# Softmax denominators through DRAM: three wide reciprocals in place of eight narrow ones

## What is computed

```
x = x + 0.5 * ffn(layernorm(x))        # silu(x Wg) * (x Wu), 2 of every 4 kept, Wd
x = x + attn(layernorm(x))
x = x + 0.5 * ffn(layernorm(x))

attn:  32 query heads of 8 channels, 8 key and value heads (4 query heads share one)
  scores = rope(q) . rope(k) / sqrt(8),  -inf above the diagonal
  out = softmax(scores) . v,  then out Wo + bo
```

## Time and profile before

| what | value |
|---|---|
| runs (3) | 810.50, 810.17, 810.17 us; median 810.17 |
| the profiled execution | 806.71 us, span 805.2 us |
| mean granted clock of PE | 0.972 |
| PE busy | 759.5 us (94%) |
| DVE busy | 716.0 us (89%) |
| ACT busy | 488.1 us (61%) |
| POOL busy | 263.5 us (33%) |
| reciprocals L1078 | 8 |

### The profile page before, as it was taken

One profiled execution on the slowest core, in us unless ns is written; L12 is line 12 of the kernel. 1 busy time (PEld: TensorE's weight loads), 2 busy tenths in 40 slices (PEclk: granted clock), 3 DMA queues, 4 the chain that ended last, 5 costly groups with the idle time before them and its releaser, 6 DMA issues.

```text
span 805.2 us, 15466 instructions
## 1 busy us (share of the span) xinstructions
PE 759.5 (94%) x5168; PEld 506.0 (63%) x5168; DVE 716.0 (89%) x1862; ACT 488.1 (61%) x949; POOL 263.5 (33%) x359
## 2 busy tenths in 40 slices
PE   4999999988899999999999999999999999999996
PEld 3787887877655544445444444544444577888886
DVE  4989999987698999999999999999995459989997
ACT  6444443321125888888888878888688544343451
POOL 1143534038732322323322223255235111533330
PEclk9999999999955999999999999999899999999999
DMA  8100000015843113333113332533313000000001
GB/s 303 55 0 1 1 1 1 1 74 179 231 147 68 41 40 75 90 74 71 43 41 75 76 73 48 141 71 78 76 35 74 14 7 1 1 27 1 27 1 52
DMA packets 21966, 48.60 MB, mean 60 GB/s; under 512 B 3744, under 2 KB 8224, under 8 KB 21376
## 3 DMA queue, kind: packets, MB, share of 16 engines
q1 hardware_dynamic: 21824, 47.56, 22.7%
q10 hardware_dynamic: 64, 0.07, 0.0%
HBM read 19.63 MB, written 14.16 MB: 42 GB/s over the span
## 4 chain that ended last, share of the span: by engine, by line
PE 64%; DVE 19%; issue 6%; POOL 5%; ACT 4%; DMA 1%; PEldq 0%; PEld 0%; SPq 0%; DVEq 0%; ACTq 0%; POOLq 0%
PE att_o_ps L1393 18%; PE att_s_ps L1377 15%; PE att_m_ps L1348 11%; PE ffn_gate L218 6%; PE ffn_up L218 5%; PE ffn_y_ps L351 5%; DVE ffn_hs L524 3%; DVE ffn_h L566 2%; POOL qkv_turned L859 2%; POOL qkv_parts L864 2%; PE att_m_ps L1356 1%; DVE att_scratch L1442 1%; DVE ffn_rank L510 1%; DVE ffn_pair_max L498 1%; PE out_y_ps L1152 1%
## 5 line engine op out<-in xcount | busy, mean ns | idle before, releaser
L1495 ACT ACTIVATE att_probs<-att_s_ps 128x512 f32<-128x512 f32 (+1 forms) x640 | 311.1, 556 | 66.3 <-PE att_s_ps L1377 64.4
L1348 PE MATMUL att_m_ps<-k,q 64*128 64x512 f32 (+3 forms) x768 | 225.1, 401 | 3.3 <-DVE att_maxima L1442 2.1
L1442 DVE CUSTOM_DVE_ANT_0 att_scratch<-att_m_ps,att_causal 128x512 bf16<-128x512 f32 (+3 forms) x512 | 221.1, 485 | 7.5 <-PE att_m_ps L1348 5.9
L1377 PE MATMUL att_s_ps<-q,k 64*128 64x512 f32 (+3 forms) x768 | 216.2, 387 | 3.3 <-ACT att_probs L1495 1.4
L1377 PEld LDWEIGHTS att_s_ps<-q,k 64*128 64x128 f32 x768 | 121.8, 190 | 101.3 <-ACT att_probs L1495 93.1
L1445 DVE TENSOR_REDUCE att_maxima<-att_m_ps 128x1 f32<-128x512 f32 x256 | 161.5, 681 | 8.0 <-PE att_m_ps L1348 8.0
L1534 POOL TENSOR_SCALAR_AFFINE_SELECT att_probs<-att_probs 128x512 f32<-128x512 f32 x128 | 80.4, 641 | 250.7 <-ACT att_probs L1495 250.7
L1393 PE MATMUL att_o_ps<-att_probs,att_vs 128*32 128x512 f32 (+3 forms) x1536 | 160.3, 505 | 2.0 <-POOL att_probs L1534 1.6
L1348 PEld LDWEIGHTS att_m_ps<-k,q 64*128 64x128 f32 x768 | 128.9, 195 | 44.8 <-DVE att_maxima L1442 25.6
L630 POOL TENSOR_TENSOR ffn_hs_lo<-ffn_hs,ffn_hs_hi 128x512 fp32r<-128x512 f32 x48 | 76.6, 1621 | 106.3 <-ACT ffn_hs_hi L427 106.3
L454 ACT ACTIVATE ffn_a<-ffn_h 128x512 f32<-128x512 f32 x64 | 40.5, 633 | 106.9 <-DVE ffn_h L566 106.9
(11 more groups left out here) (114 smaller groups left out, 1165.0 us busy)
## 6 DMA issues: line engine op xcount, KB each, us to landing
q_rows<-qkv_parts SPq DMA_DIRECT2D x16, 512.0 KB, 3.7
q<-q_rows SPq DMA_DIRECT2D x16, 512.0 KB, 4.6
q<-q SPq DMA_DIRECT2D x16, 512.0 KB, 4.4
k_rows<-qkv_parts SPq DMA_DIRECT2D x8, 256.0 KB, 3.0
k<-k_rows SPq DMA_DIRECT2D x16, 128.0 KB, 5.0
k<-k SPq DMA_DIRECT2D x16, 128.0 KB, 4.5
q<-att_shift_t SPq DMA_DIRECT2D x128, 4.0 KB
out_num<-att_sums SPq DMA_DIRECT2D x128, 16.0 KB
```

The source lines that it names most:

```text
L1348: pe.matmul(m_ps[unit_bank(n)][:, COLUMNS[m]], q[g % 2][m_lane, h, t * P:(t + 1) * P], k[g % 2][m_lane, kc * N:kc * N + cols], start=True, ...
L1377: last = pe.matmul(s_ps[n % S_BANKS][:, at:at + w], k[g % 2][s_lane, kb * P:(kb + 1) * P], q[g % 2][s_lane, h, qc * N + q0:qc * N + q0 + w ...
L1442: dve.tensor_tensor_reduce(out=scratch[bank][:, at], in0=m_ps[bank][:, at], in1=causal[:, N - n:], scale=1.0, scalar=LOWEST, op0=ALU.add, ...
L1495: act.activation(probs[u % len(probs)][:, h, SPAN[u]], s_ps[n % S_BANKS][:, SPAN[u]], ACT.Exp, scale=SCALE).then_inc(exp_done, 1)
```

## The change

The denominators of groups 0 to 11 are stored to a DRAM tensor, den_rows, in place of the SBUF tile. Two periods ahead of their use, in groups 8 and 12, SP waits for the stores of the two groups before, and issues one load that lays the 64 rows over 128 partitions x 256 columns, then the 32 rows over 128 x 128. This stands between the sums of half 0 and the next group's second shift. DVE waits for that load and inverts pieces of 128 columns as before: two behind units 6 and 12 of group 10, one behind unit 6 of group 14. The tensor of inverses has its channel dimension outermost, so that each partition's piece of a row is stored eight times with a stride; the spread reads it in that order.

```diff
@@ -986,7 +986,7 @@
-    def __init__(self, nc, ctx, late, hole, x, wo_rows, inverse_rows, KVH, QPK, HD, T, N, y_banks):
+    def __init__(self, nc, ctx, late, hole, x, wo_rows, den_rows, inverse_rows, KVH, QPK, HD, T, N, y_banks):
         self.x, self.wo_rows, self.KVH, self.QPK, self.HD, self.T, self.N = x, wo_rows, KVH, QPK, HD, T, N
         _, TILES, C = x.shape
@@ -1010,14 +1010,19 @@
         self.wo = [late.take(f"wo_{n}", [P, KT, C], F32R) for n in ("hi", "lo")]
         self.wo_raw = hole.take("wo_raw", [P, KT, C], F32)
-        self.den_rows = hole.take("out_den_rows", [self.HEADS * self.QC + self.PER_K * self.QC, N], F32)
-        self.inverse_rows = inverse_rows
+
+
+        self.den_rows, self.inverse_rows = den_rows, inverse_rows
+        self.ROW_SPANS = [slice(0, self.HEADS * self.QC), slice(self.HEADS * self.QC, (self.HEADS + self.PER_K) * self.QC)]
+        self.den_cols = [(rows.stop - rows.start) * N // P for rows in self.ROW_SPANS]
+        self.den_parts = [hole.take(f"out_den_parts{b}", [P, cols], F32) for b, cols in enumerate(self.den_cols)]
         self.y_ps = y_banks
         self.wo_loaded = sem("wo_loaded")
         self.wo_hi_ready = sem("wo_hi_ready")
         self.wo_lo_ready = sem("wo_lo_ready")
         self.stored = [[sem(f"stored{e}_{qc}") for qc in range(self.QC)] for e in range(2)]
+        self.den_loaded = [sem(f"den_loaded{b}") for b in range(2)]
         self.inverted = sem("inverted")
         self.inverse_stored = sem("inverse_stored")
         self.spread_done = [sem(f"spread_done{b}") for b in range(2)]
@@ -1066,24 +1071,29 @@
             row = self.den_row(b, k, qc) + first
             queue.dma_start(self.den_rows[row:row + self.QPK], sums[qc][HD:P:32]).then_inc(stored, 16)
+    def load_denominators(self, sp, b):
+
+        for g in ((self.KVH - 2, self.KVH - 1) if b == 0 else (self.KVH + self.KVH // 2 - 2, self.KVH + self.KVH // 2 - 1)):
+            for qc in range(self.QC):
+                self.wait_stored(sp, g, qc)
+        sp.dma_start(self.den_parts[b][:], self.den_rows[self.ROW_SPANS[b]].rearrange("r (s c) -> (r s) c", c=self.den_cols[b]))\
+          .then_inc(self.den_loaded[b], 16)
+
+    def inverse_pieces(self, b):
+        return self.den_cols[b] // self.PIECE
+
     def invert(self, dve, b, piece):
         if piece == 0:
-            for g in ((self.KVH - 2, self.KVH - 1) if b == 0 else (self.KVH + self.KVH // 2 - 2, self.KVH + self.KVH // 2 - 1)):
-                for qc in range(self.QC):
-                    self.wait_stored(dve, g, qc)
-        first = self.QC * self.HEADS
-        rows = self.den_rows[0:first] if b == 0 else self.den_rows[first:first + self.QC * self.PER_K]
-        part = rows[:, piece * self.PIECE:(piece + 1) * self.PIECE]
+            dve.wait_ge(self.den_loaded[b], 16)
+        part = self.den_parts[b][:, piece * self.PIECE:(piece + 1) * self.PIECE]
         dve.reciprocal(part, part).then_inc(self.inverted, 1)
     def store_inverse(self, sp, b):
-        sp.wait_ge(self.inverted, self.PIECES * (b + 1))
-        first = self.QC * self.HEADS
-        rows = slice(0, first) if b == 0 else slice(first, first + self.QC * self.PER_K)
-        count = rows.stop - rows.start
-        sp.dma_start(self.inverse_rows[rows], self.den_rows[rows][:, None, :].to_broadcast([count, self.HD, self.N]))\
+        sp.wait_ge(self.inverted, sum(self.inverse_pieces(n) for n in range(b + 1)))
+        columns = self.inverse_rows[:, self.ROW_SPANS[b], :].rearrange("d r (s c) -> (r s) d c", c=self.den_cols[b])
+        sp.dma_start(columns, self.den_parts[b][:][:, None, :].to_broadcast([P, self.HD, self.den_cols[b]]))\
           .then_inc(self.inverse_stored, 16)
     def spread(self, sp, b):
@@ -1093,7 +1103,7 @@
             if n == b:
                 row = self.den_row(b, k, qc)
                 sp.dma_start(self.den[:, k, self.columns(b, qc)],
-                             self.inverse_rows[row:row + self.PER_K].rearrange("h d n -> (h d) n")).then_inc(self.spread_done[b], 16)
+                             self.inverse_rows[:, row:row + self.PER_K, :].rearrange("d h n -> h d n")).then_inc(self.spread_done[b], 16)
     def split(self, pool, n):
@@ -1466,7 +1476,7 @@
                     dve.wait_ge(shift_ready, QC * (g - 1) + 1)
                 if g or m >= FIRST_SCORES:
                     m_unit(dve, g, m)
-                if g in INVERT and m in INVERT_AT:
+                if g in INVERT and m in INVERT_AT[:output.inverse_pieces(INVERT[g])]:
                     output.invert(dve, INVERT[g], INVERT_AT.index(m))
             join_maxima(g)
@@ -1636,6 +1646,8 @@
                 group_rows.copy_s(sp, g + 1)
                 load_shift(g + 1, 0)
             store_sums(g, 0)
+            if g + 2 in INVERT:
+                output.load_denominators(sp, INVERT[g + 2])
             if g < LAST:
                 load_shift(g + 1, 1)
             if g + 1 in INVERT:
@@ -1714,7 +1726,8 @@
         q_rows = nc.dram_tensor("q_rows", [C, SPLIT, B * T], F32).ap()
         k_rows = nc.dram_tensor("k_rows", [KV, SPLIT, B * T], F32).ap()
-        inverse_rows = nc.dram_tensor("inverse_rows", [3 * P // 4, HD, FIRST * P], F32).ap()
+        den_rows = nc.dram_tensor("den_rows", [3 * P // 4, FIRST * P], F32).ap()
+        inverse_rows = nc.dram_tensor("inverse_rows", [HD, 3 * P // 4, FIRST * P], F32).ap()
         N = FIRST * P
         bottom = next_free(nc)
@@ -1779,7 +1792,7 @@
         late_hole = Region(nc, hole.at)
         att_region = Region(nc, above)
         late = Region(nc, late_at)
-        output = Output(nc, ctx, late, hole, x, w_o.rearrange("(k p) n -> p k n", p=P), inverse_rows, KVH, C // HD // KVH, HD, T, N, out_ps)
+        output = Output(nc, ctx, late, hole, x, w_o.rearrange("(k p) n -> p k n", p=P), den_rows, inverse_rows, KVH, C // HD // KVH, HD, T, N, out_ps)
         attention, before_groups, first_scores, first_maxima, hooks = attention_programs(
             nc, ctx, group_rows, v, att_region, s_ps, m_ps, o_ps, output, normed2, ident_bf, x, bo, T, HD, earlier)
         between["fills"] += [lambda pool: group_rows.fill_q(pool, 0),
```

## The result

The changed kernel took 803.51 us (median of five executions, 802.92 to 806.21), the kernel before 810.17 beside it: ratio 0.9926, interval 0.9899 to 0.9953. Two later comparisons, with more executions, gave 0.9952 (0.9932 to 0.9973) and 0.9958 (0.9938 to 0.9978). So it is faster by 0.4 to 0.7%, 3.4 to 6 us. Each ratio lies nearer to the quotient of the two means than to that of the medians, so it can't be worked out from the medians given. The forecast, 804.9 after 810.17, is a ratio of 0.9935.

The account below looks back on a forecast made before the run. PE and DVE were both taken as nearly full, with eight reciprocals lengthening two periods by 7.47 us. Savings of 1.3 and 4.0 us, other terms zero, took 810.17 to 804.9 us; range 801.3 to 808.6 (8 in 10).

Parts of the forecast that it names:

- Reciprocals, first period: Group 10's period: DVE runs two reciprocals instead of four; 1.3 us goes, period 25.4 us.
- Second period: Group 14's period: one reciprocal instead of four; 4.0 us goes, period 24.9 us, counting the clock's fall as the reciprocals'.
- The load: Denominators' DMA on SP and DVE's wait for it: hidden by idle time, zero; 0.4 us at worst in the second.
- The stores of the inverses: Stores in 1024 shorter runs from 128 partitions: no change in time, zero; bounds 1.5 us sooner to 6.7 later.
- slower rival: Finer store of inverses keeps 0.143 us per packet, spread 6.7 us later, PE loses clock: 813.9 us; chance 0.05.
- The spread, zero: Reads of the stored inverses: rows of 2 KB in a new order, same bytes; cost zero.
- rival of an equal wait with a fall: Group 14: clock falls all the same behind the remaining reciprocal; 2.4 us less in all, 807.8 us; chance 0.19.
- More goes: A second clock fall behind the first four reciprocals, in runs without the profiler, goes too: 801.5 us; chance 0.13.
- The sum: Whole kernel: 1.3 + 4.0 = 5.3 us less, from 810.17 to 804.9 us; chance 0.55.

## Why the prediction was right, and where its steps failed

- **Reciprocals, first period.** Forecast 1.3 us less and 25.4; measured 26.70 - 25.51 = 1.19, and 1.36 for the two that stay, where the step had 1.34 less 0.05. Right.
- **Second period.** Forecast 24.9 us, measured 24.93 at full clock. The price of the new one, 0.8, was right, and so was that it takes the pace of the first period: it starts at partition 0. The working of the 4.0 us was wrong. "This counts the fall of the clock as caused by the reciprocals": of the 4.03 us the fall was 28.96 - 28.01 = 0.95, the three fewer reciprocals 26.70 - 24.93 = 1.77, and the start at partition 64 was 28.01 - 26.70 = 1.31. The gap of 0.04 us behind the narrow one was read, its price over four was not summed.
- **The load.** Zero, as forecast; it lands after 2.0 and 1.7 us, under the bound of 5.0. The 0.27 us in group 13 stand in no step. The changed kernel with eight reciprocals has the same load and 24.12 us there, so the load alone isn't their cause; what is stays open.
- **The stores of the inverses.** This step failed. "1.5 us sooner, which is worth nothing as PE never waits here" looked only at GpSimd and the second store. Behind the first, SP goes on to the next group's first shift, and there PE waits 0.3 to 1.5 us for it in the kernel before (periods of 24.3, 24.9 and 27.95 us) and not in the changed one (24.1). (The 24.9 is that of the kernel before with three reciprocals.) The change doesn't do away with the wait for good: one profile with the reciprocals moved has 0.48 us of it. Of the 1.7 us that the first store gains, the slower issue of the spread takes back 0.8 (2.53 us against 1.77). The 2 KB packets from 64 or 32 partitions were slow for their source: a store of 512 KB from 128 partitions in the same kernel, at 180 us, has 544 packets, nearly all of 2 KB, at (0.885 x 3.2 x 16) / 544 = 0.083 us each, against 0.143. Cut into 1 KB and 512 bytes from 128 partitions, the stores land sooner. The slower rival, with 0.143 us for each small packet, falls with this: that would have been over 9 us.
- **The spread, zero.** Its two loads in the second case take 1.23 us to issue, 0.82 before. From the issue of the store to GpSimd's quotient it is 606.93 - 599.11 = 7.82 us before and 602.17 - 594.34 = 7.83 after: the reads in the new order give back what the store gains, and GpSimd's wait stays (3.75 and 3.73 us). That the order of the reads does this was not tried by itself.
- **The clock.** The rival of an equal wait with a fall was right as a possibility: it came in one of three profiled executions of the changed kernel. "More goes" rested on a second fall behind the first four reciprocals; none was seen there in any of the profiles. The rival's price was too high: it put the fall at 807.8 - 804.9 = 2.9 us, and it took 1.2 (26.15 against 24.93); in the kernel before it was 0.95. The 3.46 us between median and profile were the spread of this kernel, of which the late shift and its fall are one part, and the 1.4 us at the end of the program another.
- **The sum.** 5.3 us against 6.7, 4.2 and 3.0 between the medians, and 3.4 to 6 by the ratios. At full clock the periods give 1.19 + 1.77 + 1.31 + 0.2 to 0.8, less 0.27 in group 13, 4.2 to 4.8 us. The term that was too large is the clock's, 0.95 of the 4.0, which one of two profiles of the kernel before has; what the DMAs' side gives, forecast at zero, fills part of its place. That the two nearly cancel is luck, and so is the first comparison, whose 6.7 us the two larger ones don't repeat.

## What to carry to other kernels

Where two engines are both full, price an instruction by its place in the queue: the same 0.95 us cost 0.3 to 0.8 us here, the full 0.8 at four of nine places. Only at one of them is the cause seen, PE's turn right behind it. When a DMA is made faster or slower, follow the queue that waits for it to its next item, and whoever waits for that. And profile the kernel before more than once when a clock fall sits in the middle of the argument: one of two profiles had it at another place.

## What the runs showed of the hardware

- A reciprocal on DVE that starts at partition 32, 64 or 96, among instructions that start at 0, doesn't overlap with its neighbours: the next one starts 0.95 to 0.98 us after it in place of 0.86, and it costs 1.1 us instead of 0.8 for the same 0.94 us. With 32, 64 or 128 partitions it is the same.
- A store from 128 partitions in 1024 runs landed in 5.4 and 3.2 us (1 MB, 512 KB); from 64 and 32 partitions in runs of 2 KB it took 7.1 and 4.4. The source and the length of the runs were changed together.
- The clock fell behind a wait of PE of 1.06 to 1.48 us in some executions and not in others. Over all profiles, behind a reciprocal at unit 6, it fell in 2 of 17 cases where that one started at partition 0 (waits of 1.06 to 1.09 us) and in 5 of 8 where it started higher (1.33 to 1.37 us).
- GpSimd's power takes 0.16 us for a column of 128 partitions (20.8 us for 128 columns). Of its 1.04 us for four columns, 0.65 would be the columns by that price.
